# Mixing stage: the first layer norm's rows made by ScalarE behind the gate sigmoid, key products ahead of the transposes

## The reference, cut to what matters

```python
x = x + attn_a(layernorm(x), ...)
x = x + ffn(layernorm(x), weight)        # ternary weights
x = x + attn_b(layernorm(x), ...)        # projections, convolutions, gates, chunked memory
x = x + ffn(layernorm(x), weight)

def layernorm(x, eps=1e-05):             # per token, over the 256 channels
    m = mean(x); v = var(x)
    return (x - m) / sqrt(v + eps)
```

## Time and profile before

| what | us |
|---|---|
| median of 3 runs (lowest, highest) | 1159.07 (1158.92, 1160.55) |
| the profiled execution, its own time | 1160.27 |
| its span, first to last instruction | 1157.8 |
| PE busy | 1065.8 (92%) |
| DVE busy | 1000.0 (86%) |
| ACT busy | 809.4 (70%) |
| POOL busy | 244.0 (21%) |

### The profile page before, as it was taken

The page is one execution under the profiler, slowest core; times in us unless marked ns, Lnnn a source line. Parts: engine busy times, 40 slices in busy tenths (PEclk is TensorE's granted clock), DMA queues, the critical chain, the costliest instruction groups (busy, mean ns, idle before and its releaser), DMA issues. The chain is left out here.

```text
span 1157.8 us, 22154 instructions
## 1 busy us (share of the span) xinstructions
PE 1065.8 (92%) x8566; PEld 586.2 (51%) x8566; DVE 1000.0 (86%) x1467; ACT 809.4 (70%) x1655; POOL 244.0 (21%) x345
## 2 busy tenths in 40 slices
PE   5997799999999999999999999995799998999995
PEld 4885233333333333333333333334567765888984
DVE  7877999999999999999999999915499998569887
ACT  4462288888888888888888888880468686343443
POOL 6514300000000000000000000014234334565643
PEclk9997599999999999999999999997899997799998
DMA  7694404413431441343144230023134325634321
GB/s 270 159 338 162 55 13 75 67 33 54 67 57 31 75 67 33 54 67 60 27 75 67 41 54 12 20 91 95 37 111 141 116 79 166 191 84 133 102 74 54
DMA packets 87332, 101.55 MB, mean 88 GB/s; under 512 B 21884, under 2 KB 57212, under 8 KB 87228
## 3 DMA queue, kind: packets, MB, share of 16 engines
q1 hardware_dynamic: 86396, 98.56, 35.3%
q10 hardware_dynamic: 832, 1.58, 0.4%
HBM read 55.09 MB, written 43.88 MB: 85 GB/s over the span
## 5 line engine op out<-in xcount | busy, mean ns | idle before, releaser
L653 ACT ACTIVATE prob<-ps_s 128x512 f32<-128x512 f32 x1024 | 555.7, 597 | 115.1 <-PE ps_s L723 97.7
L674 DVE TENSOR_REDUCE maxes<-ps_m 128x2 f32<-128x1024 f32 x512 | 606.6, 1218 | 17.8 <-PE ps_m L712 14.6
L735 PE MATMUL ps_o<-prob,v_ones 128*32 128x256 f32 x4096 | 327.8, 392 | 7.8 <-issue 6.7
L723 PE MATMUL ps_s<-q_stack,k_stack 64*128 64x512 f32 x1024 | 261.0, 499 | 0.0
L712 PE MATMUL ps_m<-k_stack,q_stack 62*128 62x512 f32 x1024 | 219.2, 422 | 14.7 <-DVE maxes L674 11.0
L723 PEld LDWEIGHTS ps_s<-q_stack,k_stack 64*128 64x128 f32 x1024 | 99.7, 184 | 211.3 <-ACT prob L653 186.7
L735 PEld LDWEIGHTS ps_o<-prob,v_ones 128*32 128x32 f32 x4096 | 81.6, 108 | 191.6 <-issue 100.8
L615 POOL COPY v_ones<-v_all 128x512 f32<-128x512 f32 x16 | 9.8, 614 | 531.1 <-PE ps_o L735 531.1
L712 PEld LDWEIGHTS ps_m<-k_stack,q_stack 62*128 62x128 f32 x1024 | 101.0, 192 | 31.6 <-DVE maxes L674 23.5
L69 DVE BATCH_NORM_STATS2 p_stats<-x_all 128x6 f32<-128x256 f32 x124 | 43.5, 413 | 6.7 <-DMA x_all<-in_x_dram 5.9
L1138 DVE TENSOR_TENSOR x_all<-x_all,p_a 128x512 f32<-128x512 f32 x16 | 10.9, 681 | 42.9 <-POOL p_pre_q L971 30.5
(11 more groups left out here) (276 smaller groups left out, 1497.0 us busy)
## 6 DMA issues: line engine op xcount, KB each, us to landing
qk_parts<-p_parts SPq DMA_DIRECT2D x32, 512.0 KB, 7.1
q_stack<-qk_parts SPq DMA_DIRECT2D x96, 128.0 KB, 4.7
k_stack<-qk_parts SPq DMA_DIRECT2D x96, 128.0 KB, 7.8
oT<-o_sb SPq DMA_DIRECT2D x32, 256.0 KB, 3.9
x_all<-in_x_dram SPq DMA_DIRECT2D x8, 512.0 KB, 10.2
heads<-oT SPq DMA_DIRECT2D x16, 256.0 KB
inverse<-inverse_sums SPq DMA_DIRECT2D x16, 256.0 KB
out_dram<-x_all SPq DMA_DIRECT2D x7, 512.0 KB, 3.4
```

Source lines behind the costliest of these rows:

```text
L653: act.activation(prob[at % P_RING][:, h], ps_s[:, (GH * at + h) % S_RING], ACT.Exp, scale=HD ** -0.5).then_inc(exp_done, 1)
L674: dve.tensor_reduce(maxes[:, i // 2, i % 2], ps_m[:, i % M_PAIRS], AX.X, ALU.max).then_inc(m_taken, 1)
L723: pe.matmul(ps_s[:, (GH * (UNITS * slot + KT * qc + kt) + h) % S_RING], r32(k_st[slot][rows, pair, kt * P:(kt + 1) * P]), r32(q_st[slot][r ...
L735: ins = pe.matmul(ps_o[32 * h:32 * h + 32, queries], v_st[slot][:, kt, h], prob[(UNITS * slot + KT * qc + kt) % P_RING][:, h, queries], st ...
```

## The change

z is no longer made by DVE but by ACT, as scale times x plus shift, with scale = rstd and shift = -mean x rstd. For the shift POOL gets two more small instructions per chunk (`negative_means`), right behind the first norm's `deviation`. On ACT the four instructions of `put_z` stand between the two sigmoids: the second one is taken out of `project_copies` and becomes `theta_sigmoid`. On DVE `put_z` disappears. On PE `key_products` moves in front of `turn_z`. Nothing else moves, and no data type changes.

```diff
+    shift = sb("shift", [P, 2, TPC])
...
+        def negative_means(n):
+            pool.wait_ge(rstd_z, n + 1)
+            pool.tensor_tensor(tmp[:, n % 2, 0], mv[:, n % 2, 0, :, 0], rstd[:, n % 2, 0], ALU.mult).then_inc(shift_steps, 1)
+            pool.wait_ge(shift_steps, n + 1)
+            pool.tensor_tensor(shift[:, n % 2], scalar(const, S_ZERO, [P, TPC]), tmp[:, n % 2, 0], ALU.subtract).then_inc(shift_ready, 1)
...
             if valid(it + 3):
                 deviation(it + 3, 0, var_z, rstd_z)
+                negative_means(it + 3)
...
             act.activation(sig_ea[:], ps_p[:, 2], ACT.Sigmoid, bias=cols[:, COL_GATE_B:COL_GATE_B + 1]).then_inc(p_taken, 1)
+
+        def theta_sigmoid(n):
             act.wait_ge(sig_ready, 2 * n + 1)
             act.activation(sig_t[HI], sig_t[HI], ACT.Sigmoid).then_inc(sig_ready, 1)
+
+        def put_z(n):
+            act.wait_ge(shift_ready, n + 1)
+            if n:
+                act.wait_ge(zT_turned, n)
+            for i in range(TPC):
+                ins = act.activation(z[:, i], x_of(n)[:, i], ACT.Identity, bias=shift[:, n % 2, i:i + 1], scale=rstd[:, n % 2, 0, i:i + 1])
+            ins.then_inc(z_ready, 1)
...
             if valid(it + 1):
                 project_copies(it + 1)
+            if valid(it + 3):
+                put_z(it + 3)
             if valid(it + 1):
+                theta_sigmoid(it + 1)
                 oldest_taps(it + 1)
...
-        def put_z(n):
-            dve.wait_ge(rstd_z, n + 1)
-            if n:
-                dve.wait_ge(zT_turned, n)
-            normalise(dve, x_of(n), mv[:, n % 2, 0], rstd[:, n % 2, 0], z, z_ready)
-
...
-            if valid(it + 3):
-                put_z(it + 3)
...
             if valid(it + 1):
                 gate_means(it + 1)
+            if valid(it):
+                key_products(it)
             if valid(it + 3):
                 turn_z(it + 3)
-            if valid(it):
-                key_products(it)
```

More of the change, by code:

```diff
@@ L845, in mix @@
     scanned, k2_ready, aqb_ready, kce_ready, zeros_set = map(sem, ("scans", "k_norms", "aqb", "kce", "zeros_set"))
+    shift_ready, shift_steps = sem("shift_z"), sem("shift_steps")
     q_dup = [sem("q_doubled0"), sem("q_doubled1")]
```

## The result

The changed kernel takes 1181.34 us (median of 4 runs, 1179.76 to 1186.63) against 1159.22 for the kernel before: 22.1 more, a ratio of 1.0195 with the interval 1.0166 to 1.0223. The sign was forecast, the size was not: 1173.8 was the forecast and 1179 the end of the range. The profiled execution took 1182.1, with a span of 1180.0 against 1157.8. All rows are of one profiled execution of each kernel.

A forecast was written before the change was run, and what follows sets the result against it. ACT's queue from L1008 to L1072 was taken as part of the loop, PE's nearly as long. Queue 11.9, start 1.25 and clock 1.5 gave 14.7, on the median 1159.07: 1173.8 us, range 1170.5 to 1179.

The forecast's parts named there:

- The sign: Whole kernel: slower at 0.95, the same at 0.03, faster at 0.02.
- The bound: Mixing-stage loop: ACT's queue L1008 to L1072 (12.48 us) is part of it; PE nearly as long, DVE follows.
- The queue's term: ACT between L1014 and L1016: four z instructions hold the queue 1.98 us in six iterations, 11.9 in all (11.4 to 12.6).
- GpSimd's two instructions: POOL behind rstd: the shift is ready before ACT asks for it, so cost 0, with 0.1 as the other end.
- The swap: PE, key products before z's transposes: hides the later z, where PE would stand 1.0; by itself changes nothing else.
- The start: Stage's start, it = -3: the path to z(0) grows by 0.55 on POOL and 0.7; 1.25 passes through (0.9 to 3.0).
- The clock: PE's new 1.7 us pause before theta: one fall, expected in it = 4, costing 1.5; none in the other five.
- The ticking clock: Rival, chance 0.19: each of the six pauses before theta brings a fall; three to six of 1.5 give 1176.7 to 1181.2.

The follow-up runs named there:

- swap and GpSimd's work: Kernel before plus key products ahead of the transposes of z and two GpSimd instructions per chunk, z still on VectorE: 1173.44 us, ratio 1.0117.
- two needless instructions: Kernel before plus two ScalarE instructions computing nothing needed, between the two sigmoids, about 1.0 us: 1166.78 us, ratio 1.0077.
- three needless instructions: Kernel before plus three ScalarE instructions computing nothing needed, between the two sigmoids, about 1.5 us: 1170.82 us, ratio 1.0101.
- four needless instructions: Kernel before plus four ScalarE instructions computing nothing needed, between the two sigmoids in six iterations, about 2.0 us: 1180.05 us, ratio 1.0175.
- needless work behind `copy_hT`: Kernel before plus four ScalarE instructions computing nothing needed, behind copy_hT, where ScalarE then waits for the projections: 1159.33 us, ratio 1.0015.

## Why the prediction was wrong, point by point

- **The bound.** Right: ScalarE's queue from L1008 to L1072 is in the loop. The 0.72 stayed, 2 us cost their full length and the falls of the clock between the sigmoids and nothing behind `copy_hT`, and VectorE's relief gave nothing.
- **The queue's term.** Right: 1.98 per iteration was priced, 1.97 measured in the queue, and 1.96 and 1.81 by turns in the iteration once the clock is held. In the iterations of 1.81 some 0.15 fell on ScalarE's wait for the transposes (`copy_zT` started 0.85 behind L1030 there, 0.71 in the others), which I had put at 0.04 at most. Without the clock's part the six iterations grew by 19.6 - 8.2 = 11.4, against 11.9.
- **GpSimd's two instructions.** Right: the shift was ready 1.1 early, and alone they cost nothing.
- **The swap.** Half right: z waited for nothing in a full iteration. In it = -1 there are no key products, so PE stood 0.83 for z, under the longer wait at theta. "The swap by itself changes nothing else" held only where z is late. What I didn't see is that it gathers the idle time: 5 to 7 us dearer than the same kernel without it.
- **The start.** Priced 1.25, measured 2.2. z(0) came 1.31 later, as worked out. The rest, 0.9, lies between the second `out_products` of the stage and the first projections, with `out_products` of 4.91 and 4.56 instead of 4.35 and 4.34: 25.58 where the kernel before took 24.68. In the seven runs above that leave this stretch and all ahead of it as before, it took 24.76 to 26.99, so the 0.9 can't be put down to the change.
- **The clock.** This is the step that failed: "I take **1.5** for one fall, and none in the other five". All six iterations had one. Five cost 1.5 to 1.7 each, together 8.2, and the sixth 2.76, together 11.0 where 1.5 stood. Some 1.7 came back behind the stage. So the number of falls was wrong. The price of one was right for `out_products`, and too low by 1.3 for the one fall that was forecast, in it = 4, where the projections bore it. The text took single pauses of 1.25 and 1.47 that had left the clock alone as a bound for the length that does harm. They were pauses in other surroundings, and none was a sample of repeated ones. With a pause of 1.25 the run with the swap and GpSimd's work had three falls in four full iterations.
- **The rival.** The ticking clock, at 0.19, is what happened, and its 1176.7 to 1181.2 nearly holds the 1181.3. What the Trainium skill (TensorE: Matmul & The Clock Gate, A second HAM failure mode: psum-queue depth-cycling) tells of another kernel, a clock that goes up and down with short idles between groups of matmuls, is what the changed kernel's trace shows in kind: PEclk is 0.93 in each of its three full iterations shown, with one fall in each. The idles there come from another cause, and the page gives no length for them. I held against it that iterations with 0.48 of idle kept 1.00. That was true and did not bear on pauses three times as long.

## What to carry to other kernels

Before moving work to the engine with the most idle time, ask where in its iteration that time lies: an engine that idles in one block in front of a wait and runs without a break behind it can be the bound at 73% busy. A new pause of TensorE is priced twice, once for the wait and once for the clock behind it, and here the second price fell on the next dense matmuls, which lay in the same loop. Where such a pause can't be avoided, try to keep work in it or to split it: a reorder that hides one wait by joining it to another can be the dearer choice.

## What the runs showed of the hardware

- A pause of TensorE ahead of theta that comes back in each iteration brought falls of the clock far below the 2.37 of rows 8. In one profiled execution of each kernel, of the `out_products` of the four full iterations (it = 0 to 3) these were slow:

| kernel | pauses ahead of theta | slow, of four |
|---|---|---|
| two needless instructions | 0.29, 0.61 | 0 |
| changed, without the swap | 0.44, 0.77 (and 0.83 at the transposes) | 1 |
| three needless instructions | 0.80, 1.15 | 2 |
| swap and GpSimd's work | 1.25 | 3 |
| four needless instructions | 1.34, 1.68 | 3 |
| changed | 1.38, 1.72 | 4 |

- The length alone doesn't decide it. In it = -1 pauses of 1.99 and 2.52 left the clock alone, while two of 2.15 and one of 3.05 brought a fall. The 1.25 there brought none in the kernel before and one in the run with needless work behind `copy_hT` (0.50 in 839 to 841, the iteration 1.67 longer). In that same run the projections behind it = 4 took 7.11, with the same waits as in the kernel before, where they took 5.42. What else decides it is not shown here.
- One fall cost 1.69 in `out_products` (5.38 for 3.69) and 1.69 to 2.89 in the projections (7.11, 8.18 in the changed kernel, and 8.31, for 5.42).
- More matmuls made a kernel faster: 1.8 us of repeated work per iteration took the changed kernel from 1181 to 1174.
